# Expert numbers read once per stretch, and index, value products and second norm put into other steps, in a fused attention and expert kernel

## The reference, cut to what matters

```python
x = x + attn_a(layernorm(x), w_qkv, w_out, rel_bias)   # x is 8 x 256 x 128, 16 heads of 64, softmax over 256 with bias
x = x + ffn(layernorm(x), Wr, br, ln_g, ln_b, W1, b1, W2, b2)
x = x + attn_b(layernorm(x), w_kv_down, w_kv_up, w_q, w_out)  # causal, keys and values through a latent of 128
x = x + ffn(layernorm(x), Wr, br, ln_g, ln_b, W1, b1, W2, b2)

def ffn(x):                          # per token, 8 experts, the best one is taken
    probs = softmax(x @ Wr + br);  gate = max(probs);  idx = argmax(probs)
    xn = layernorm(x) * ln_g + ln_b
    h = relu(xn @ W1[idx] + b1[idx])      # 128 -> 512
    return (h @ W2[idx] + b2[idx]) * gate # 512 -> 128
```

## Time and profile before

| | us |
|---|---|
| median of 3 runs | 693.21 |
| lowest and highest run | 689.38 and 693.81 |
| the profiled execution, its own time | 694.63 |
| its span, from the first to the last instruction | 693.4 |
| mean granted TensorE clock in it | 0.988 of full |
| PE, ACT, DVE and POOL busy | 655.1, 534.2, 471.9, 361.1 |

### The profile page before, as it was taken

One profiled execution on the slowest core, in us unless ns is written; L12 is line 12 of the kernel. 1 busy time (PEld: TensorE's weight loads), 2 busy tenths in 40 slices (PEclk: granted clock), 3 DMA queues, 4 the chain that ended last, 5 costly groups with the idle time before them and its releaser, 6 DMA issues.

```text
span 693.4 us, 17716 instructions
## 1 busy us (share of the span) xinstructions
PE 655.1 (94%) x5406; PEld 551.3 (80%) x5406; DVE 471.9 (68%) x2113; ACT 534.2 (77%) x1768; POOL 361.1 (52%) x672
## 2 busy tenths in 40 slices
PE   6899999999999999999898999999999999989894
PEld 5678787888888888779796787888788888868893
DVE  3876767676777767966354668687768668896433
ACT  3788888788888879765664989898989889874462
POOL 3344635465556555636462446465745655644552
PEclk9999999999999999999998999999999999999998
DMA  9999999920000000014220000000000000020214
GB/s 265 193 182 180 211 248 182 183 38 6 1 6 5 9 1 10 24 40 151 79 63 16 2 1 3 1 1 6 14 2 1 10 10 1 17 47 17 78 31 127
DMA packets 71212, 42.71 MB, mean 62 GB/s; under 512 B 7953, under 2 KB 68254, under 8 KB 70864
## 3 DMA queue, kind: packets, MB, share of 16 engines
q1 hardware_dynamic: 66336, 36.31, 27.5%
q0 software_dynamic: 2624, 4.23, 1.9%
q10 hardware_dynamic: 2160, 1.05, 0.6%
HBM read 17.68 MB, written 25.06 MB: 62 GB/s over the span
## 4 chain that ended last, share of the span: by engine, by line
PE 79%; DVE 10%; issue 4%; ACT 3%; DMA 1%; POOL 1%; SPq 0%; DVEq 0%; POOLq 0%; ACTq 0%
PE ps L419 15%; PE ps L565 13%; PE ps L528 13%; PE ps L414 9%; PE ps L416 8%; PE ps L415 8%; PE ps L668 6%; PE ps L682 5%; DVE ring L1151 3%; ACT ring L857 1%; PE ps L602 1%; DMA wkn<-in_w_qkv 1%; ACT f_ht L906 1%; PE ps L620 1%; POOL ys_scratch L322 1%
## 5 line engine op out<-in xcount | busy, mean ns | idle before, releaser
L315 POOL TENSOR_SCALAR ring<-ring,rs 128x256 f32<-128x256 f32 (+1 forms) x500 | 220.0, 458 | 219.7 <-DVE rs L1162 218.7
L857 ACT ACTIVATE ring<-ring,mn 128x256 f32<-128x256 f32 (+1 forms) x512 | 243.4, 488 | 0.0
L419 PE MATMUL ps<-ident,ring 128*128 128x128 f32 x896 | 121.8, 275 | 3.7 <-POOL ring L315 2.4
L528 PE MATMUL ps<-qk 64*128 64x256 f32 (+1 forms) x1024 | 115.0, 363 | 0.2 <-ACT qk L825 0.2
L565 PE MATMUL ps<-pt,v 128*64 128x256 f32 (+1 forms) x1024 | 111.9, 359 | 2.0 <-DVE pt L1178 1.3
L419 PEld LDWEIGHTS ps<-ident,ring 128*128 128x128 f32 x896 | 102.2, 142 | 11.1 <-POOL ring L315 3.5
L857 ACT ACTIVATION_READ_ACCUMULATOR ring<-ring,mn 128x1 f32 x512 | 104.1, 203 | 0.0
L565 PEld LDWEIGHTS ps<-pt,v 128*64 128x64 f32 x1024 | 65.8, 136 | 46.2 <-issue 13.1
L528 PEld LDWEIGHTS ps<-qk 64*128 64x128 f32 x1024 | 82.6, 187 | 18.3 <-issue 8.5
L825 ACT COPY qk<-ps 128x512 f32<-128x512 f32 x128 | 74.8, 585 | 28.4 <-PE ps L416 26.9
L1151 DVE CUSTOM_DVE_ANT_0 ring<-ps,cm 128x128 f32<-128x128 f32 (+1 forms) x256 | 73.6, 350 | 6.3 <-PE ps L528 6.2
(11 more groups left out here) (209 smaller groups left out, 1339.2 us busy)
## 6 DMA issues: line engine op xcount, KB each, us to landing
xs_scratch<-padt SPq DMA_DIRECT2D x16, 1032.0 KB, 18.5
w<-in_W SPq DMA_DIRECT2D x16, 256.0 KB, 5.4
f_xs<-xs_scratch SPq DMA_DIRECT2D x50, 64.5 KB, 2.0
xs_scratch<-padt SPq DMA_DIRECT2D x2, 838.5 KB, 16.7
T<-in_bias SPq DMA_DIRECT2D x2, 512.0 KB, 8.2
T<-in_bias SPq DMA_DIRECT2D x1, 1024.0 KB, 11.1
bu<-in_w_kv_up SPq DMA_DIRECT2D x1, 1024.0 KB, 7.9
ys_scratch<-f_ys,f_xs POOLq DMA_INDIRECT x50
```

The lines of the kernel that those rows point to most:

```text
L315: i = pool.tensor_scalar(ring[:, hh, it, 0:w], ring[:, hh, it, 0:w], rs[:, q], 1.0, ALU.mult, ALU.mult)
L419: return pe.transpose(out, src, ident[:, :])
L528: i = pe.matmul(PS[u % 2][hh][:, 256 * it:256 * it + w], qk[rows, 128 * it:128 * it + 128], qk[rows, 256:256 + w], start=True, stop=True)
L857: i = act.activation(ring[:, hh, it, 0:w], ring[:, hh, it, 0:w], ACT.Exp, bias=mn[:, q], scale=-1.0, accum_out=sm[:, q])
```

## The change

- `experts` becomes one list that PE and DVE fill by one `load` of 12 values at tile 0 and one of 5 at tile 20, where there were loads of 4, 4, 4, 4 and 1 (for the own tiles no load was made). Three loads fewer on PE and three on DVE in each chunk.
- `INDEX`: part 1 moves from step 62 to 63, part 3 from 76 to 77; its second half is a new part 4 in step 79. From step 73 on, `routes` stands behind the bias additions and `W` in DVE's step, not ahead.
- `XT(0)` moves on PE from step 64 to step 65, behind `TR(61)`; `H(0)` moves behind `PV(60)`, `PV(61)` and `out_last` of the same step.
- Chunk 0's start: the transposes and the split of the value weights go behind the first scores, the four quarters of batch 0's values go to steps 3, 3, 6 and 8 (before 2, 3, 4, 4), and the norm of batch 1 one step later.

```diff
-VALUES = [{2: [(0, 0)], 3: [(0, 2)], 4: [(0, 1), (0, 3)]}, {0: [(0, 0)], 1: [(0, 2)], 2: [(0, 1)], 4: [(0, 3)]}]
+VALUES = [{3: [(0, 0), (0, 2)], 6: [(0, 1)], 8: [(0, 3)]}, {0: [(0, 0)], 1: [(0, 2)], 2: [(0, 1)], 4: [(0, 3)]}]
...
-INDEX = {60: 0, 62: 1, 65: 2, 76: 3}
+INDEX = {60: 0, 63: 1, 65: 2, 77: 3, 79: 4}
...
     b = at(s, PRE[part])
+    if st == 0 and (b == 1 or at(s - 1, PRE[part]) == 1):
+        return 1 if b is None else None
     return b if b else None
...
         def Y(n):
-            if own(n) is not None:
-                experts[n % 4] = own(n)
-            elif n in FIRST_OF:
-                experts[0:4] = load(mybir.EngineType.PE, f_ei, *GROUPS[FIRST_OF[n]], NE - 1)
-            e = experts[n % 4]
+            if n in (0, F_MORE):
+                experts[:] = load(mybir.EngineType.PE, f_ei, n, NF if n else K0, NE - 1)
+            e = own(n)
+            if e is None:
+                e = experts[n if n < K0 else n - F_MORE]
...
             if 0 <= s < NU:
                 QK(s)
-            if st == 0 and s == 0:
-                value_weights()
...
-            if 0 <= n < NF:
+            if n == 0:
+                XT(0)
+            if 1 <= n < NF:
                 H(n)
...
                 S(s)
+            if st == 0 and s == 1:
+                value_weights()
             if s % 2 and 5 <= s < NU + 4:
                 PV(s - 5)
                 PV(s - 4)
             if s in LAST:
                 out_last(*LAST[s])
+            if n == 0:
+                H(n)
...
             if st == 0 and s == 1:
-                value_weights()
                 products(3)
...
-            if s > NU:
+            if NU < s <= LAST_POST["place"]:
                 routes(s)
...
-            if s <= NU:
+            if not NU < s <= LAST_POST["place"]:
                 routes(s)
```

More of the change, by code:

```diff
@@ L33 @@
 NG = len(GROUPS)
-FIRST_OF = {a: g for g, (a, b) in enumerate(GROUPS)}
 GROUP_OF = {n: g for g, (a, b) in enumerate(GROUPS) for n in range(a, b)}
@@ L48 @@
 QUARTERS = (0, 2, 1, 3)
-VALUES = [{2: [(0, 0)], 3: [(0, 2)], 4: [(0, 1), (0, 3)]}, {0: [(0, 0)], 1: [(0, 2)], 2: [(0, 1)], 4: [(0, 3)]}]
+VALUES = [{3: [(0, 0), (0, 2)], 6: [(0, 1)], 8: [(0, 3)]}, {0: [(0, 0)], 1: [(0, 2)], 2: [(0, 1)], 4: [(0, 3)]}]
 for _v in VALUES:
-    _v |= {8 * b + 2 * i - 2: [(b, n)] for b in range(1, NB) for i, n in enumerate(QUARTERS)}
-VALUE_NO = {(b, n): 4 * b + i for b in range(NB) for i, n in enumerate(QUARTERS)}
+    for _b in range(1, NB):
+        for _i, _n in enumerate(QUARTERS):
+            _v.setdefault(8 * _b + 2 * _i - 2, []).append((_b, _n))
+VALUE_NO = [{q: i for i, q in enumerate(q for s in sorted(v) for q in v[s])} for v in VALUES]
 NY = 8
@@ L443, in pe_steps @@
     def pe_steps(st):
-        experts = [None] * 4
+        experts = []
         causal = st == 1
@@ L473, in values @@
         def values(b, n):
-            k = 4 * B0 + VALUE_NO[(b, n)] + 1
+            k = 4 * B0 + VALUE_NO[st][(b, n)] + 1
             j, half_ = n // 2, n % 2
@@ L557, in PV @@
             if c in (0, 4):
-                pe.wait_ge(a_vs, 4 * B0 + VALUE_NO[(b, 2 + c // 4)] + 1)
+                pe.wait_ge(a_vs, 4 * B0 + VALUE_NO[st][(b, 2 + c // 4)] + 1)
             if U0 + u and u % 2 == 0:
@@ L749, in step @@
             for g in range(NG):
-                if n == max(GROUPS[g][0] - 2, -1) and GROUPS[g][0] != F_EACH:
+                if n == GROUPS[g][0] - 2 and GROUPS[g][0] not in (0, F_EACH):
                     XT(g)
@@ L796, in inputs_free @@
                 act.wait_ge(t_t, 8 * g + 8)
-                act.wait_ge(t_v, 4 * (g // NB * NB) + VALUE_NO[(g % NB, 3)] + 1)
+                act.wait_ge(t_v, 4 * (g // NB * NB) + VALUE_NO[g // NB][(g % NB, 3)] + 1)
         def pre_b(b):
@@ L829, in values @@
             r = slice(512 * half_, 512 * half_ + 512)
-            act.wait_ge(t_v, 4 * B0 + VALUE_NO[(b, n)] + 1)
+            act.wait_ge(t_v, 4 * B0 + VALUE_NO[st][(b, n)] + 1)
             if B0 + b >= 2:
@@ L952, in step @@
             if st == 0 and s == 1:
+                products(3)
                 value_weights()
-                products(3)
             if s % 2 and 3 <= s < NU:
@@ L974, in step @@
                 out(b)
-            if n == F_EACH:
+            if n in (0, F_EACH):
                 XT(GROUP_OF[n])
@@ L1285, in index @@
                 ends_of(more, ends)
+            if part == 4:
                 g, g2 = f_g[:, 0:NX1, :], f_g2[:, 0:NX1, :]
@@ L1301, in W @@
                 dve.wait_ge(d_w, 16 * D_W)
-            if n in FIRST_OF:
-                experts[0:4] = load(mybir.EngineType.DVE, f_ei, *GROUPS[FIRST_OF[n]], NE - 1)
-            e = experts[n % 4]
+            if n in (0, F_MORE):
+                experts[:] = load(mybir.EngineType.DVE, f_ei, n, NF if n else K0, NE - 1)
+            e = experts[n if n < K0 else n - F_MORE]
             if dyn(n) >= 4:
@@ L1389, in step @@
                 S(s)
+            if st == 0 and s == 1:
+                value_weights()
             if s % 2 and 3 <= s < NU:
                 weigh(s - 2)
+            if st == 0 and s in (0, 2, 4, 6):
+                biases(s)
             if (b := pre_at(s, "a", st)) is not None:
                 pre_a(b)
-            if st == 0 and s in (0, 2, 4, 6):
-                biases(s)
             if s == LAST_KEEP:
```

## The result

The changed kernel takes 701.05 us (median of 4 runs, 699.91 to 701.39), the kernel before 693.36 on the same chip (689.38 to 693.81). The ratio is **1.0126**, 95% interval 1.0098 to 1.0153: 8.7 us slower by the ratio, 7.7 by the medians. That is more than the 1% within which the prediction had put a chance of 0.60; it had given 0.37 to slower. The profiled run took 700.82, its span is 699.6 us (before 693.4), its mean granted clock 0.981 (before 0.988).

The account below looks back on a forecast made before the run. PE, busy 94%, was taken as the bound. On 694.63 us, +2.9 and +2.2 (index), 2 x 1.6 (clock), 2 x -0.75 (split) and -0.4 (start) gave +6.4, so 699.6 us on the median; range 689.5 to 704.

Parts of the forecast that it names:

- The index behind the scores: Between attention and experts, later index part 1 delays fetched rows, XT(0) and step 66: +2.9 us chunk 0, +2.2 chunk 1.
- The clock: At both transitions, idle PE falls to its lower clock and resumes at half rate for 3.1 us: +1.6 us per chunk.
- rival 2: At both transitions, a long clock fall, 6.4 us at half rate in each chunk: 702.8 us, chance 0.15.
- Putting H(0) last does not help: In step 65, H(0) last hides ACT's copy of XT(0), but XT(0) stays ahead of 3.8 us of attention work.
- The split: At tile 11, index part 3 behind the additions lets Y(11) follow XT(3) sooner: -0.75 us in each chunk.
- The loads: On PE and DVE, three fewer expert-number loads per chunk bring nothing; twelve values take about 0.41 us.
- Rival 4: Ahead of W(0) and Y(0), each loaded value costs 0.32 us, some 5 us per chunk: 709.6 us, chance 0.04.
- The start: At chunk 0's start, value weights go behind the first scores: -0.4 us, taken between -1.4 and +0.1.
- Rival 1: At both transitions, the waits come but PE's clock does not fall: 696.4 us, chance 0.20.
- rival 3: At both transitions, early scores win if SP's fetch needs at most 2.2 us; they cost nothing: 690.3 us, chance 0.14.

Follow-up runs that it names:

- e8_fill: The change with 18 and 13 transposes that nobody reads put into PE's two waits of step 65: 697.16 us, ratio 1.0072 to the kernel before.
- e2_place: The kernel before with only index part 1 in step 63, XT(0) behind TR(61) and H(0) at the end of step 65: 696.93 us, ratio 1.0143.
- e5_index62: The change with index part 1 back in step 62, PE's and ACT's new order kept: 691.28 us, ratio 1.0052 to the kernel before.
- e9_keep_first: The change with relu(0) on ACT moved from step 65 to 66, behind keep of units 60 and 61: 700.02 us, ratio 1.0110 to the kernel before.
- e6_split: The kernel before with only index part 3 split and put behind the bias additions (steps 77 and 79): ratio 1.0002.
- e1_start: The kernel before with only the change's new start of chunk 0: 687.56 us, ratio 0.9991.
- e13_both60: The kernel before with the new start and index part 1 directly behind part 0 in step 60: 689.28 us, ratio 0.9956.
- e3_back: The change with index part 1 back in step 62 and XT(0), H(0) in their old places: 687.79 us, ratio 1.0003 to the kernel before.

## Why the prediction was right, step by step

**The index behind the scores, +2.9 and +2.2.** Right in kind, half too large: without the clock the waits cost 2.05 and 1.32 (e8_fill). Two rows account for 0.95 us of chunk 0. `f_ri` was done 6.67 us behind `S(62)`, not 7.18, because the index ran faster at its new place, 1.75 us to `f_ri` instead of 2.40: before, the second `f_g` instruction of 128 x 96 takes 0.66 us beside POOL's work on `xn`, in the change 0.26, and an `f_e` one of 128 x 8 takes 0.42 and 0.17:

```profile
289.09 0.26 DVE L1266 TENSOR_TENSOR f_g<-iota_s,f_e 128x96 f32<-128x96 f32 x1
289.39 0.66 DVE L1267 TENSOR_TENSOR f_g<-f_g,f_e 128x96 f32<-128x96 f32 x1
```

```profile
289.11 0.82 POOL L344 TENSOR_TENSOR xn<-xn,lnb 128x256 f32<-128x256 f32 x1
```

```profile
292.06 0.26 DVE L1274 TENSOR_TENSOR f_g<-f_g,f_e 128x96 f32<-128x96 f32 x1
```

The Trainium skill, page "SBUF — State Buffer", section "SBUF: two separate sides", has a DVE instruction with two SBUF inputs and a GpSimd instruction that reads SBUF share one pair of ports as a lock held for a whole instruction. These rows agree: the slow `f_g` ends at 290.05, 0.12 us behind POOL's instruction. And from `f_ri` to `XT(0)` it took 4.32 us, not 4.76. My line to call it right, `XT(0)` waiting more than 2 us, was missed: it waits 1.46 and 1.69. In chunk 0 I had 2.5 us (298.4 to 300.9). `TR(61)` ended 9.53 us behind `S(62)`, almost as I had it (9.43), but the rows were there 0.94 sooner. `TR(61)`'s second half stood 2.31 us, where I had about 3, so PE stood 3.8 us in these two waits and not 5.5.

**The clock, 2 x 1.6.** Right for the change's trace: 1.56 and 1.49 by e8_fill. In e2_place, with the same order, chunk 1's transition is 0.72 us longer still, again by when the clock fell. It fell in both chunks of all five profiled kernels with the index in step 63 and no filler. It stayed low for 6.8 us, so in length it was rival 2's fall, which I had priced at 3.2 in each chunk. It cost half of that: PE stood for part of this time, and the 0.46 us that `TR(61)`'s half lost is hidden in `XT(0)`'s wait for its rows. What is left in chunk 0 is `XT(0)`, 1.09 instead of 0.62, and the `PV` row, 3.02 instead of 1.95. That my 3.1 us of half rate gave the same price is luck in part.

**"Putting H(0) last does not help."** The step that failed: I put this move at nothing. I asked what `H(0)` at the end of the step gains, not what it had been covering and who stands behind it. It filled PE's wait for DVE's copy (1.47 instead of 0.58 us, e5_index62), and through relu(0) it held `keep`, which makes `TR(62)` to `PV(62)` 0.99 and 1.19 us longer (e9_keep_first). These last two are +2.18 that my sum did not have; with ACT's order mended they go in the rows, while the ratio is 1.0110 on its chip against 1.0126, with intervals that overlap.

**The split, 2 x -0.75.** Wrong: nothing that could be measured. `Y(11)` follows `XT(3)` as said, and `H(14)` takes it back (e6_split). I named nothing that is late next there, though ACT's relu was.

**The loads, 0.** Right in time. The size was off: "twelve take about 0.41 us" drew a line from one load of four values through to twelve, and they take 1.04 to 1.10. Loads of four take 0.34 to 0.59 us in the same trace, so the row I took was one of the quick ones; from one value (0.32) to twelve it is some 0.07 us for each further value (0.61 for five). The Trainium skill's 200 ns for each register (page "Runtime: NRT & Kernel Launch", "Instruction fetch mechanics") would give 2.4 us, an estimate; no row here reaches half of it. Rival 4 falls.

**The start, -0.4.** Not contradicted: -0.6 us with an interval from -1.9 to +0.6, which takes in nothing as well. The profile alone would have said -2.8 and that I was wrong; one trace is one draw of the moment from which PE runs at full rate. PE is not idle from 23 to 25 us, as said.

**The sum.** Predicted +6.4, measured +7.7 by the medians. Too much for the waits (-1.7), too little for `H(0)` (+2.2), no gain from the split (+1.5): errors that partly cancel, so that the sum came this near is luck in part. Rival 1 and rival 3 fall with the clock and the waits in every trace of that order. Rival 3 had the right test: SP's fetch does need over 4 us.

## What to carry to other kernels

When the late engine's work is put later to let other work pass, count all that stands behind it there; in a stretch where that engine has no idle time, look for its idle time ahead instead (here two steps earlier, for 0.4% gained where the change lost 1.3%). Before a product is moved, ask which wait it fills and whose queue its consumer heads. A span difference ahead of the place that was changed may be chance in the start: take it from timed rounds, not from two traces.

## What I had not expected

The expert layer's time depends on the chip more than on any of these edits. From `PV(62)` to the last `Y` it takes 51.83 and 51.65 us in e1_start's trace, where the kernel before runs at 687.45, and 54.14 and 54.16 in e13_both60's, same code there, where it runs at 692.18. In the longer traces a relu or an addition around tiles 7 to 11 starts 1 to 2 us behind the product that it needs, and the rows name as releaser only that product, or nothing of this core; what held it stays open. Within one chip this stretch differs by up to 1.2 us between the traces, between chip A and the other two by 1.0 to 3.7. PE standing 2.3 us and then, soon behind, 0.8 to 2.0 us more brought its clock down for 6.8 us or more in both chunks of five kernels, in eight of these ten places before the second wait had begun; 31 transposes of 0.12 us in these waits kept it up and delayed neither `TR(61)` nor `XT(0)`. But it also fell once in e3_back and once in e5_index62, behind waits of 0.9 us that elsewhere left it alone, so a fall can't be read from the waits with certainty.
